# Transfers in the order of need, and every fourth state product on GpSimd, in a hybrid attention, FFN and Mamba kernel

## What is computed

```python
x = x + attn_a(layernorm(x))     # gated delta rule, 16 heads of 128
x = x + ffn(layernorm(x))        # w_down(silu(w_gate x) * w_up x), 256 -> 1024 -> 256
x = x + attn_b(layernorm(x))     # Mamba, below
x = x + ffn(layernorm(x))
# attn_b: D_INNER 512, STATE 16
xn = rmsnorm(x) * norm_w;  x_inner, z = split(xn @ in_proj_w.T)
u = silu(conv4(x_inner) + conv_b)
B, C, dt = split(u @ x_proj_w.T);  dt = softplus(dt * dt_w + dt_b)
def step(h, (dt_t, B_t, C_t, u_t)):
    h = exp(dt_t * A) * h + (dt_t * u_t) * B_t
    y_t = sum(h * C_t, state axis) + D * u_t
out = (y * silu(z)) @ out_proj_w.T + x
```

## Time and profile before

| | us |
|---|---|
| median of 3 runs | 2563.15 |
| profiled execution | 2566.89 |
| its span in the trace | 2565.1 |
| TensorE busy | 2276.0 (89%) |
| VectorE busy | 2009.3 (78%) |
| ScalarE busy | 1719.9 (67%) |
| GpSimd busy | 1186.5 (46%) |

### The profile page before, as it was taken

How to read it: one execution, slowest core, us unless ns; L and a number is a source line. 1 busy time by engine, 2 the same in 40 slices (tenths; PEclk the granted TensorE clock), 3 DMA queues, 4 the chain that set the end, 5 groups by cost and what they waited for, 6 DMA issues and landing times.

```text
span 2565.1 us, 87271 instructions
## 1 busy us (share of the span) xinstructions
PE 2276.0 (89%) x38320; PEld 1337.3 (52%) x38320; DVE 2009.3 (78%) x3095; ACT 1719.9 (67%) x3491; POOL 1186.5 (46%) x940
## 2 busy tenths in 40 slices
PE   6689999999999999999999999998658878878677
PEld 3456666666666666666666666665323322323223
DVE  3768888888888887887887878885357879999981
ACT  2667788778878786776777778876635757655432
POOL 0445544554555454544334445452045465747630
PEclk8889999999999999999999999999878989899889
DMA  1000000000000000000001000000351152434400
...
DMA packets 49707, 91.08 MB, mean 36 GB/s; under 512 B 7852, under 2 KB 17836, under 8 KB 48816
## 3 DMA queue, kind: packets, MB, share of 16 engines
...
## 4 chain that ended last, share of the span: by engine, by line
PE 51%; DVE 23%; ACT 11%; issue 10%; POOL 2%; SPq 1%; DMA 1%; POOLq 0%; DVEq 0%; ACTq 0%
PE bank L396 8%; PE bank L500 5%; DVE cv L708 4%; DVE bank L1904 4%; PE pair L623 4%; PE bank L467 4%; PE bank L657 3%; PE pair L611 3%; PE bank L593 2%; PE bank L436 2%; ACT Y L1084 2%; DVE kq L796 2%; DVE R L798 2%; PE pair L1583 2%; PE bank L616 2%
## 5 line engine op out<-in xcount | busy, mean ns | idle before, releaser
L708 DVE SCALAR_TENSOR_TENSOR cv<-raw,taps,cv 128x1024 f32<-128x1024 f32 x288 | 396.5, 1377 | 20.3 <-ACT cv L972 18.5
L2263 POOL TENSOR_TENSOR dBu<-dtu_wide,Bn 128x1024 f32<-128x1024 f32 x128 | 300.9, 2363 | 229.7 <-DVE bank L1904 207.0
L396 PE MATMUL bank<-xn,W 128*128 128x512 f32 x768 | 372.0, 615 | 0.0
L1268 POOL TENSOR_TENSOR kq<-kq,tot 128x512 f32<-128x512 f32 x128 | 218.9, 1710 | 210.6 <-PE bank L467 210.6
L1245 POOL TENSOR_TENSOR R<-kq,gate 128x1024 f32<-128x1024 f32 x32 | 77.5, 2423 | 487.7 <-ACT gate L1038 487.7
L2151 ACT ACTIVATE bank<-dt_wide,m_A 128x512 f32<-128x512 f32 x256 | 172.8, 688 | 121.2 <-DVE hc L1912 80.7
L396 PEld LDWEIGHTS bank<-xn,W 128*128 128x128 f32 x768 | 135.9, 193 | 121.7 <-issue 113.2
L1904 DVE TENSOR_TENSOR_SCAN bank<-bank,dBu 128x512 f32<-128x512 f32 x128 | 152.8, 1218 | 49.4 <-ACT bank L2151 34.5
L971 ACT ACTIVATE raw<-bank 128x512 f32<-128x512 f32 x192 | 114.9, 598 | 103.0 <-PE bank L396 100.7
L1270 POOL TENSOR_TENSOR R<-R,tot 128x512 f32<-128x512 f32 x128 | 164.3, 1284 | 0.0
L1904 DVE TENSOR_TENSOR_SCAN bank<-bank,carry,dBu 128x512 f32<-128x512 f32 x128 | 159.1, 1277 | 3.0 <-ACT bank L2151 2.3
...
## 6 DMA issues: line engine op xcount, KB each, us to landing
...
```

Source lines behind the costliest of these rows:

```text
L396: m = pe.matmul(psum[bank][:, :], w[:, (kind * KT + k) * P:(kind * KT + k + 1) * P], xn[:, k, b, cols], start=k == 0, stop=k == KT - 1)
L708: dve.scalar_tensor_tensor(cv[m % 2][:, :, :], raw[m % 2][:, :, i:i + SEG], taps[:, h, KQV[n], i:i + 1], cv[m % 2][:, :, :], MUL, ADD).the ...
L1268: pool.tensor_tensor(Lv[:, :, 0, :], Lv[:, :, 0, :], spread(two[:, :, 1], 2, half), MUL).then_inc(up_l.sem)
L2263: pool.tensor_tensor(dBu[at % AHEAD][:, :, :], dtu_wide[n % 2][:, half * DT2:(half + 1) * DT2, :], spread(Bn[sg][:, :], 1, DT2), MUL).then ...
```

## The change

- Unit 0's loads are issued in this order: half of dtu (two of four quarters of tile 0), B of group 0, half of dt, C of group 0, the other halves, rows(1), w_gate, rows(2), w_up, rows(3), w_down, wide(1), w_o. The first halves, w_up and w_down get semaphores of their own (old ones, with the counts they have by then). TensorE waits for w_gate ahead of the gates, w_up ahead of the ups, w_down ahead of the down products.
- Item q = 3 of each group: VectorE's scan reads the PSUM bank and writes to a new SBUF tile `hs` (one buffer). VectorE no longer multiplies it with C; GpSimd does, into the same place in hc, at the step of that item, after the dBu issued ahead of it. VectorE waits before it writes hs: for GpSimd's product of the group before and, in units 0 and 1, for ScalarE's copy of its carry. ScalarE's `carry_out` waits for the scan alone there. TensorE's gather and SyncE's reload of C wait for both VectorE's three and GpSimd's one.
- All places of FRONT_AT, FFN_AT and EARLY_AT are drawn anew. Among them, for w = 1: step 4 from 95.7 to 107.1, step 5 from 101.2 to 110.8, step 13 from 116.1 to 118.6.

The diff, with the tables cut:

```diff
--- before.py
+++ after.py
@@ -54,52 +54,52 @@
 FRONT_STEPS, FFN_STEPS = 44, 26
 FRONT_AT = [
-    [131.5541, 135.0487, 135.0487, 137.3885, 138.9477, 140.2744, 140.2744, 160.6999, 163.1809, 163.1809, 163.1809,
...
-     177.6396, 178.9781, 178.9781, 178.9781, 178.9781, 178.9781, 178.9781, 186.4895, 187.93, 190.7263, 192.6478],
...
-    [277.926, 285.797, 285.797, 287.8189, 289.7481, 289.7481, 301.9528, 313.4958, 318.2594, 319.1472, 319.1472,
...
+    [131.2355, 132.8791, 132.8791, 135.1998, 135.1998, 139.2887, 139.2887, 141.9285, 142.2719, 143.6525, 143.6525,
...
+     170.3487, 170.7386, 170.7386, 176.389, 176.389, 176.389, 178.2052, 180.9687, 180.9687, 180.9687, 184.3684],
...
+    [281.1734, 285.325, 290.0258, 300.4449, 304.3425, 311.7361, 311.7361, 324.4582, 324.4582, 326.7614, 330.9562,
...
 FFN_AT = [
-    [-52.4215, 64.2648, 64.2648, 64.2648, 95.7294, 101.226, 102.3558, 103.379, 107.7599, 110.9792, 110.9792,
-     112.425, 112.5156, 116.0603, 120.1501, 120.1501, 120.5198, 123.1916, 123.2461, 123.3898, 124.739, 125.9745,
...
+    [-287.4832, -227.1858, -93.9686, -40.7158, 107.0681, 110.7753, 111.7997, 114.2974, 114.2974, 114.2974,
+     116.6526, 116.6526, 118.5503, 118.5503, 120.6712, 120.6712, 120.674, 120.674, 124.9184, 124.9184, 124.9184,
...
@@ -309,7 +309,7 @@
         prod_full, na_set = tally("prod_full", NL + 1), tally("na_set", NL)
         rk_set, rq_set = tally("rk_set"), tally("rq_set_then_dBu_set")
         bsI_set, level = tally("bsI_set", 2), tally("level", NL)
-        up_t, up_l, up_k = tally("up_t_then_dt", NL), tally("up_l", NL), tally("up_k", NL + 1)
+        up_t, up_l, up_k = tally("up_t_then_dt", NL), tally("up_l_then_hc_later", NL), tally("up_k", NL + 1)
         up_t1, up_l1, up_q = tally("up_t1"), tally("up_l1"), tally("up_q_then_mu")
         e0_set, e_set, et_set = tally("e0_set", 2), tally("e_set", NL - 1), tally("et_set", NL)
         inv_full, um_set = tally("inv_full", NL), tally("um_set", NL - 1)
@@ -1410,6 +1410,7 @@
         Bn = [sm(f"Bn{i}", [P, SEG]) for i in range(SG)]
         Cn = [sm(f"Cn{i}", [P, SEG]) for i in range(SG)]
         dBu = [sm(f"dBu{i}", [P, DT2, SEG]) for i in range(AHEAD)]
+        hs = [sm(f"hs{i}", [P, SEG]) for i in range(1)]
         hc = [sm(f"hc{i}", [P, DT2, SEG]) for i in range(BACK - 1)] + [cen]
         mb.close()
 
@@ -1445,8 +1446,11 @@
         c_in = [tally(f"C{i}_in") for i in range(SG)]
         dt_wide_in = [tally(f"dt_wide{i}_in") for i in range(2)]
         dtu_wide_in = [tally(f"dtu_wide{i}_in") for i in range(2)]
+        dt_first_in, dtu_first_in, up_loaded, down_loaded = eye_loaded, x_loaded, small_loaded, mamba_loaded
+        DT_FIRST, DTU_FIRST, UP_LOADED, DOWN_LOADED = 16 + QS * 16, 16 + QS * 16, 8 * 16 + 16, 10 * 16 + 16
         dA_set, dBu_set, h_set = kRT_set.after(NG, 1), rq_set.after(NG, 1), d_set.after(NG, 1)
-        hc_set, gathered, carry_set = s_set.after(NG, DT2), pred_full.after(NG, 1), tally("carry_set", ITEMS)
+        hc_set, gathered, carry_set = s_set.after(NG, QS - 1), pred_full.after(NG, 1), tally("carry_set", ITEMS)
+        hc_later = up_l.after(NG, 1)
         y_gated, out_full, m_added = x_added.after(NG, DT), tally("out_full", KT), tally("m_added", KT)
 
         FFN_DVE = 2
@@ -1577,7 +1581,7 @@
                     bank = take()
                     if j == 0:
                         if w == 1:
-                            pe.wait_ge(ffn_loaded.sem, (3 * NJ + 3) * 16)
+                            pe.wait_ge(ffn_loaded.sem, (3 * NJ + 1) * 16)
                         pe.wait_ge(*xh_set(w))
                     for k in range(KT):
                         m = pe.matmul(psum[bank][:, :], wg[:, k, j * P:(j + 1) * P], xh[:, k, :], start=k == 0,
@@ -1588,6 +1592,8 @@
                 yield
                 for j in range(NJ):
                     bank = take()
+                    if w == 1 and j == 0:
+                        pe.wait_ge(up_loaded.sem, UP_LOADED)
                     for k in range(KT):
                         m = pe.matmul(psum[bank][:, :], wu[:, k, j * P:(j + 1) * P], xh[:, k, :], start=k == 0,
                                       stop=k == KT - 1)
@@ -1599,6 +1605,8 @@
                     bank = take()
                     if k == 0:
                         pe.wait_ge(*hid_set.at(w, NJ - 1))
+                        if w == 1:
+                            pe.wait_ge(down_loaded.sem, DOWN_LOADED)
                     for j in range(NJ):
                         m = pe.matmul(psum[bank][:, :], wd_cols(j, k), hid_of(j), start=j == 0, stop=j == NJ - 1)
                     m.then_inc(down_full.sem)
@@ -1682,7 +1690,8 @@
 
             def gather(n, sg):
                 group = n * SG + sg
-                pe.wait_ge(*hc_set.at(2 * group + 1, DT2 - 1))
+                pe.wait_ge(*hc_set.at(group, QS - 2))
+                pe.wait_ge(*hc_later.at(group))
                 for q in range(QS):
                     m = pe.matmul(psum[Y_BANKS[n % 2]][quad(q), :], sel[:, :],
                                   hc[(2 * group + q // DT2) % BACK][:, q % DT2, :], start=False, stop=sg == SG - 1,
@@ -1901,13 +1910,21 @@
                         if seg and i == 0:
                             dve.wait_ge(*carry_set.at(b, ITEMS - 1))
                     h = psum[A_BANKS[at % NA]]
-                    dve.tensor_tensor_scan(h[:, :], h[:, :], dBu[p % AHEAD][:, jj, :],
+                    kept = h[:, :]
+                    if q == QS - 1:
+                        group = at // QS
+                        kept = hs[0][:, :]
+                        if group >= 1:
+                            dve.wait_ge(*hc_later.at(group - 1))
+                            if (group - 1) * QS < NB * ITEMS:
+                                dve.wait_ge(*carry_set.at(0, (group - 1) * QS + QS - 1))
+                    dve.tensor_tensor_scan(kept, h[:, :], dBu[p % AHEAD][:, jj, :],
                                            carry[:, b, i:i + 1] if seg else 0.0, MUL, ADD).then_inc(h_set.sem)
                     if jj == DT2 - 1:
                         dve.wait_ge(*rows_loaded(c_in, u, sg))
                         if p >= BACK:
                             dve.wait_ge(*gathered.at((p - BACK) // 2))
-                        for k in range(DT2):
+                        for k in range(DT2 if q == 1 else DT2 - 1):
                             dve.wait_ge(*h_set.at(p * DT2 + k))
                             dve.tensor_tensor(hc[p % BACK][:, k, :], psum[A_BANKS[(p * DT2 + k) % NA]][:, :],
                                               Cn[sg][:, :], MUL).then_inc(hc_set.sem)
@@ -2133,10 +2150,15 @@
             def carry_out(at):
                 u, i = divmod(at, ITEMS)
                 seg, b = divmod(u, NB)
-                act.wait_ge(*hc_set.at(at // DT2, at % DT2))
+                group, q = divmod(at, QS)
+                if q == QS - 1:
+                    act.wait_ge(*h_set.at(at))
+                    ends = hs[0]
+                else:
+                    act.wait_ge(*hc_set.at(group, q))
+                    ends = psum[A_BANKS[at % NA]]
                 if seg == 0:
-                    act.activation(carry[:, b, i:i + 1], psum[A_BANKS[at % NA]][:, SEG - 1:SEG],
-                                   ACT.Copy).then_inc(carry_set.sem)
+                    act.activation(carry[:, b, i:i + 1], ends[:, SEG - 1:SEG], ACT.Copy).then_inc(carry_set.sem)
                     act.wait_ge(*carry_set.at(u, i))
 
             def decay(u, i):
@@ -2144,7 +2166,9 @@
                 at, n = u * ITEMS + i, u * DT + j
                 if i == 0 and u == 0:
                     act.wait_ge(*mA_ready.at(0))
-                if sg == 0 and q == 0:
+                if n == 0 and sg == 0 and q == 0:
+                    act.wait_ge(dt_first_in.sem, DT_FIRST)
+                elif sg == 0 and q == (0 if n else DT2):
                     act.wait_ge(*tile_loaded(dt_wide_in, n))
                 if at >= NA:
                     carry_out(at - NA)
@@ -2255,7 +2279,9 @@
                 def feed(p):
                     j, sg, half = pair_of(p)
                     at, n = u * PAIRS + p, u * DT + j
-                    if sg == 0 and half == 0:
+                    if n == 0 and sg == 0 and half == 0:
+                        pool.wait_ge(dtu_first_in.sem, DTU_FIRST)
+                    elif sg == 0 and half == (0 if n else 1):
                         pool.wait_ge(*tile_loaded(dtu_wide_in, n))
                     pool.wait_ge(*rows_loaded(b_in, u, sg))
                     if at >= AHEAD:
@@ -2270,6 +2296,15 @@
                         p = i // DT2
                         if p + LEAD < PAIRS:
                             feed(p + LEAD)
+                    if i % QS == QS - 1:
+                        at = u * ITEMS + i
+                        group, p = at // QS, at // DT2
+                        pool.wait_ge(*rows_loaded(c_in, u, item_of(i)[1]))
+                        if p >= BACK:
```

(63 more changed lines are left out.)

38 lines of the change are left out of this document (19 added, 19 removed), and 36 rows, old and new, of tables (EARLY_AT, FRONT_AT).

## The result

The changed kernel takes 2517.8 us, median of four runs (2515.8 to 2524.8), beside 2562.3 for the kernel before (2560.1 to 2564.9): ratio 0.9831, 95% interval 0.981 to 0.9852. (The kernel before has one run more here than ahead of the prediction.) The prediction was 2515 us, range 2492 to 2542. The profiled execution took 2518.0 us, its span is 2516.3 us.

What follows compares the result with a forecast made beforehand. VectorE bounds units 1 to 3; unit 0 starts with a stall of program order. Gains of 20 (start), 10 (rest of unit 0) and 18 (units 1 to 3) make 48 us: 2566.9 to 2518.9, less 3.7 for the median, 2515 us; range 2492 to 2542.

Steps and rivals of the forecast that it cites:

- Start, 20 us: Up to item 14's scan: 20 us gained, bounds 15 and 24; first scan 5.6 us earlier, SiLU wait some 12 us.
- Attention, 0 us: Early places (first FFN, front(0)) move by a fraction of a head: 0 us, bounds -2 and +2.
- Rest of unit 0, 10 us: Item 14 to unit 1: 6 of the 8.67 us handover wait and 4 of 7.1 us of multiplications gained.
- Units 1 to 3, 18 us: 28.3 us of multiplications leave VectorE, less 10 us of new idle (bounds 3 and 25): 18 us gained.
- the term of 28.3: VectorE in units 1 to 3: 48 multiplications fewer at 0.59 us each, 28.3 us.
- End, 0 us: After 2492.8 us, mostly the last tile's second FFN: not touched by the change, 72 us as now.
- Product, scan, conv: GpSimd product 1.2 us; scan into SBUF costs 0 extra; conv steps held beside GpSimd cost 1 to 2 us.
- the slower rival: GpSimd holds the scans into hs in SBUF, 1.2 us each, 77 in all: 29 us slower, 2592 us; chance 0.05.
- while GpSimd is on time: New waits of VectorE, SyncE and TensorE's gather cost nothing then; about ten exceptions in units 1 to 3, 1 us each.
- The redrawn places ease this stretch: GpSimd's nearly gapless work from 2184.1 to 2222.4 us: two front steps leave items 121 and 129 for 135.

Runs made afterwards that it cites:

- the transfers alone: Kernel before with only unit 0's new load order and a semaphore for each FFN weight; VectorE multiplies all, old places: 2545.5 us, ratio 0.9937.
- the small product: Changed kernel, but from the fourth group on GpSimd's product covers 8 columns instead of 512: 2513.7 us, ratio 0.9807.
- The swaps: Kernel with new loads, GpSimd product and old places (2582.7 us); on GpSimd alone, the product moved ahead of front and FFN steps at five places: 2571.0 us, ratio 1.0032.

## Why the prediction was right, step by step

**Time and range.** 2515 against 2517.8. Term by term, with the table of stages:

- **Start, 20 us: right.** From the first wide load to the first scan 16.3 us before, 12.4 after, 3.8 less; the stage to item 14 went from 52.4 to 36.2, 16.2 less; together 20.0. Two errors inside it cancel: I had 5.6 and 14.4. With the early places of before and the new loads, the first part takes 10.6 to 12.1 (six kernels), a gain of 4.2 to 5.6; the new early places cost up to 1.8 in this part, where I gave them nothing. The SiLU cost VectorE 3.7 us, not 12, but decays held it 1.5 + 2.8 + 2.2 ahead of that. By the table the transfers alone give 16 of the 20, the redrawn places 5, and the product takes 1.
- **Attention, 0 us.** 6.1 in the trace, and not from the change: seven kernels with the attention order of before issued the first wide load at 1839.2 to 1844.9, and the kernel before at 1846.45; the six with the new order at 1840.3 to 1844.1. It goes with TensorE's granted clock at the start, between 100 and 200 us. In the four profiles with the latest load its mean there was 0.90 or 0.91 (0.90 in the kernel before), in the ten others 0.94 to 0.98 (0.94 in the changed kernel). The clock changes between 2.4 and 1.2 GHz there, and stood at 1.2 longer in those four. Why, no run shows.
- **Rest of unit 0, 10 us: right.** Measured 9.3 (150.6 to 141.3). The places gave 7.4, of it 6.5 at the handover (8.38 to 1.91 us; I counted 6), and the product 1.6, where I counted 4. The places also cost: the unit's 12 conv steps take 15.8 us, 10.0 before. (My working counts 12 fourth items behind item 14; there are 13, which is 0.6 us.)
- **Units 1 to 3, 18 us: too much.** Measured 10.6 (11.4 to the end of the last products, as in the rows by stage). VectorE's busy time fell by 404.0 - 374.7 = 29.3 us, as the term of 28.3 said. The new idle is 17.9 instead of 10: this is the mis-sized term, and its cause was wrong too. I gave it to GpSimd's being late, with ScalarE's decay as a small part of it; VectorE's direct waits for dBu are 0.4 us, for the product none. It waits for ScalarE's decay (14.5 us, 8.9 before), a SiLU and the output product. What upstream makes these late I haven't traced. Without the product VectorE idles 24.4 us between the same two scans, with it 39.8; and with the small product this part is 401.7 us. So up to 11 of the 18 go with GpSimd's time in the product after all, though by way of other engines. (The steps 5 and 6 that my working gives to front(2) are those of front(3).)
- **End, 0 us.** 2.8, unexplained; over all kernels this part is 72.4 to 77.4 us.
- **Product, scan, conv.** 1.27 and not 1.2 us; the scan into hs is not held (1224 ns at most without, 1284 with carry, beside 1232 and 1294 into PSUM), so the slower rival has no ground. The conv step L1847 has a median of 752 and a maximum of 2884 ns (1975 before). The Trainium skill, "SBUF — State Buffer", section "SBUF: two separate sides", fits both: that step reads two SBUF inputs, the scan one. I priced this at 1 to 2 us. The 36 conv steps behind the first scan take 32.7 us before, 36.5 with the new places and loads alone, 37.6 in the changed kernel: the product costs 1.1 us of it there. With the old places it costs 8.1 (32.7 to 40.8).

**What the prediction missed.** It weighed the product by whose queue is free (5.8 against 6.3 us per group) and by dBu behind it. It said that the gather's wait costs nothing "while GpSimd is on time", and priced the exceptions at 1 us. With the old places one exception cost 7.5 us and the held conv steps 8, and the whole product turned from 37.8 us of freed VectorE time into 36 us lost. The new places were not a side matter but what makes this part of the change pay. "The redrawn places ease this stretch" was right in kind, but had no price, and no rival asked what the product costs where the places do not fit it. That the sum fits the traces is luck: 48 us were forecast and 48.8 measured, because the 7.4 us missing in units 1 to 3 stood against 6.1 of a long attention part in the profile that the sum started from, and 2.8 at the end. Without the attention part the traces differ by 42.7 us, and the medians by 44.5. I had taken 3.7 us off, by which that profile stood above its median; against the medians the forecast is 2.8 us too low. The range was wide enough for any of this.

Left open: most of the 48 us. The swaps give 11, the conv steps some 7 (8.1 less 1.1). Not tried apart is which of FRONT_AT and FFN_AT carries the rest, and not run are the new places without the new transfers. TensorE's granted clock is a rival for a part: its mean in units 1 to 3 is 0.88 with product and old places, 0.89 without the product, and with the new places 0.94 and 0.92. TensorE is busy there 339.0, 332.0, 330.0 and 339.9 us. Whether the clock is cause or effect no run shows.
